# Decoder layer: y's last transposes behind a V sum, query weights split ahead of q's copy, the first half's last additions divided between engines, dt projection of half 1 as one fp32r matmul

## What is computed

```python
# x: (8,128,512), ctx: (8,128,512)
h  = layernorm(x)
xp = h @ xp_w.T                       # 16 columns dt, 16 B, 16 C
dt = softplus(xp[..., :16] @ dt_w.T + dt_b)
# scan over the 128 tokens, 16 states a channel
s_t = exp(dt_t * A) * s_{t-1} + dt_t * B_t * h_t ;  y_t = sum_n s_t * C_t + D * h_t
x  = x + y
z  = layernorm(x); z = z * rsqrt(mean(z*z) + eps) * ln_w
q, k, v = z @ w_q.T, ctx @ w_k.T, ctx @ w_v.T      # 32 heads of 128
x  = x + softmax_masked(q k^T + bias) v @ w_out.T
x  = x + x_ln @ W.T + b + sum_e probs[e] * (x_ln @ A_e^T) @ B_e^T
```

## Time and profile before

| | before |
|---|---|
| median of 3 runs | 916.41 us |
| lowest, highest | 914.9, 916.72 us |
| the profiled execution | 916.63 us |
| its span | 914.8 us |
| PE busy | 904.4 us (99%) |
| DVE, ACT, POOL busy | 697.0, 515.9, 663.8 us |
| mean granted TensorE clock | 0.996 |
| the chain that ended last | PE 87%, DVE 10%, POOL 1% |
| PE's waits that the trace names, the longest three | 2.9 us (line 618, for DVE's y), 1.5 us (line 537, at the start), 1.3 us (line 666, for DVE's `q_sb`) |

### The profile page before, as it was taken

How to read it: one execution, slowest core, us unless ns; L and a number is a source line. 1 busy time by engine, 2 the same in 40 slices (tenths; PEclk the granted TensorE clock), 3 DMA queues, 4 the chain that set the end, 5 groups by cost and what they waited for, 6 DMA issues and landing times.

```text
span 914.8 us, 15425 instructions
## 1 busy us (share of the span) xinstructions
PE 904.4 (99%) x5150; PEld 778.9 (85%) x5150; DVE 697.0 (76%) x763; ACT 515.9 (56%) x1188; POOL 663.8 (73%) x429
## 2 busy tenths in 40 slices
PE   9999999999999998999999999999999999999998
PEld 8687688888888887888899999999899999999876
DVE  5699997999999999456666676676666677767774
ACT  3686868576665675365655555555555555555330
POOL 3247788997678776457698878788878888787522
PEclk9999999999999999999999999999999999999999
DMA  9555476675777753356554444545454545454302
GB/s 310 166 156 166 143 230 184 204 208 183 215 238 229 241 171 126 110 170 226 162 169 157 137 158 135 158 136 158 137 159 135 158 135 160 134 169 136 109 1 93
DMA packets 96849, 150.26 MB, mean 164 GB/s; under 512 B 10576, under 2 KB 35280, under 8 KB 96672
## 3 DMA queue, kind: packets, MB, share of 16 engines
q1 hardware_dynamic: 86432, 131.54, 44.3%
q10 hardware_dynamic: 10368, 18.09, 7.9%
HBM read 113.81 MB, written 35.78 MB: 164 GB/s over the span
## 4 chain that ended last, share of the span: by engine, by line
PE 87%; DVE 10%; POOL 1%; issue 1%; ACT 0%; DVEq 0%; ACTq 0%; POOLq 0%
PE acc L508 11%; PE acc L510 11%; PE acc L509 11%; PE misc L510 6%; PE misc L508 6%; PE misc L509 6%; PE acc L789 6%; PE acc L734 6%; PE acc L666 5%; PE acc L667 5%; PE acc L668 5%; DVE misc L1225 4%; PE acc L758 3%; DVE w L1232 2%; DVE misc L1220 2%
## 5 line engine op out<-in xcount | busy, mean ns | idle before, releaser
L1486 POOL TENSOR_TENSOR y<-y,w 128x2048 f32<-128x2048 f32 x31 | 143.5, 4630 | 58.4 <-DVE w L1232 57.4
L1225 DVE TENSOR_TENSOR_SCAN misc<-dA,misc 128x2048 f32<-128x2048 f32 x32 | 141.7, 4429 | 4.3 <-ACT dA L862 1.1
L1083 ACT ACTIVATE prob<-prob,negm 128x128 f32<-128x128 f32 x256 | 99.9, 391 | 41.6 <-DVE negm L1295 41.6
L1090 ACT ACTIVATE ot_hi<-acc 128x512 fp32r<-128x512 f32 x64 | 38.3, 599 | 143.3 <-PE acc L789 143.3
L1547 POOL TENSOR_TENSOR wt_lo<-ws,wt_hi 128x1024 fp32r<-128x1024 f32 x27 | 65.1, 2410 | 61.7 <-ACT wt_hi L1071 61.7
L508 PE MATMUL misc<-wo_hi,ot_hi 128*128 128x512 f32 x256 | 107.1, 418 | 0.5 <-POOL wo_lo L1564 0.5
L510 PE MATMUL misc<-wo_hi,ot_lo 128*128 128x512 f32 x256 | 101.3, 396 | 0.0
L508 PE MATMUL acc<-wv_hi,ctx_hi 128*128 128x512 f32 x256 | 101.2, 395 | 0.0
L509 PE MATMUL misc<-wo_lo,ot_hi 128*128 128x512 f32 x256 | 100.8, 394 | 0.0
L510 PE MATMUL acc<-wv_hi,ctx_lo 128*128 128x512 f32 x256 | 100.0, 391 | 0.0
L509 PE MATMUL acc<-wv_lo,ctx_hi 128*128 128x512 f32 x256 | 99.9, 390 | 0.0
(11 more groups left out here) (196 smaller groups left out, 2438.6 us busy)
## 6 DMA issues: line engine op xcount, KB each, us to landing
k_scratch<-kst SPq DMA_DIRECT2D x64, 256.0 KB, 3.6
bc<-xp_scratch ACTq DMA_DIRECT2D x32, 512.0 KB, 5.7
v_scratch<-vst SPq DMA_DIRECT2D x32, 512.0 KB, 4.2
k_sb<-k_scratch SPq DMA_DIRECT2D x64, 256.0 KB, 2.9
v_sb<-v_scratch SPq DMA_DIRECT2D x64, 256.0 KB, 2.7
wo_raw<-in_wo SPq DMA_DIRECT2D x64, 256.0 KB, 2.9
wp<-in_wq SPq DMA_DIRECT2D x54, 256.0 KB, 3.8
wraw<-in_wk SPq DMA_DIRECT2D x32, 256.0 KB, 5.0
```

The source lines that it names most:

```text
L1083: last = act.activation(prob[q][:, b], prob[q][:, b], ACT.Exp, bias=negm[q][:, b:b + 1], accum_out=psum[q][:, b:b + 1])
L1225: dve.tensor_tensor_scan(h_ps, flat(dA[k % 2][:, :, :, :]), h_ps, 0.0, ALU.mult, ALU.add).then_inc(da_free, 1)
L1486: pool.tensor_tensor(y_half(half), y_half(half), w[:, k % 2], ALU.add).then_inc(y_ready, 1)
```

## The change

Five parts.

1. **dt projection.** In half 1 it was one fp32 matmul over 16 rows. It becomes one fp32r matmul over 96 rows: three blocks at partitions 0, 32 and 64 hold the low part of xp with the rounded dt weights, then rounded with rounded, then rounded xp with the low part of the weights; the rows between are zero. For that POOL sets `dtw` and `xp3` to zero (`rows_set`), SP loads dt_w three times, ACT's `xp_slot` has one copy of 96x512 and three of 16x512 ahead of its copy of 48x512, and POOL has two subtractions of 16x512 (`low_xp`) behind its addition of step 1. PE's first dt projection waits for the second.
2. **T_DT** goes from 85 to 23, by which `due` moves exponentials on ACT and `low_w` on POOL.
3. **V sum ahead of y's last transposes.** V sum 0 of the last group stands ahead of them; four stand between them and z's transposes as before, and one instead of two in `behind(0)`.
4. **`split_wq(g + 1)`** stands ahead of the copy of q on ACT in the plain steps.
5. **Divided additions.** Of the four of `add_sums(0)`, DVE keeps two. For the other two, ACT copies bank times `anykey` to `o_sum`, and POOL adds it to `base`.

```diff
-KZ = 12
-Y_AT = KP
+Y_AT = KP + 1
+KZ = KP + 5
...
-T_SUM, T_TR, T_XP, T_DT, T_EXP = 273, 45, 340, 85, 234
+T_SUM, T_TR, T_XP, T_DT, T_EXP = 273, 45, 340, 23, 234
...
+            sp.wait_ge(rows_set, 1)
+            for i in range(3):
+                sp.dma_start(dtw[32 * i:32 * i + R], a["dt_w"]).then_inc(dtw_in, 16)
...
             def dt_proj(half, c, out):
 
-                return pe.matmul(out, dtw[:, c * P:(c + 1) * P], xp_sb[0:R, half], start=True, stop=True)
+                cols = slice(c * P, (c + 1) * P)
+                if half:
+                    return pe.matmul(out, dtw3[0:R3, cols], xp3[0:R3], start=True, stop=True)
+                return pe.matmul(out, dtw[0:R, cols], xp_sb[0:R, 0], start=True, stop=True)
...
             pe.wait_ge(w_lo_done, 3)
+            pe.wait_ge(xp_lo_done, 1)
             for c in range(C):
                 pe.wait_ge(sum_evac, max(bank_free(DT[c]), XP + 1))
                 dt_proj(1, c, acc[:, bank_of(DT[c])]).then_inc(sum_done, 1)
...
             k_group(NG - 1)
+            v_group(NG - 1, range(1))
             for b in range(HB):
                 pe.wait_ge(y_ready, NSTEP + b)
                 y_transpose(HB + b, misc[:, b]).then_inc(yt_ps, 1)
-            v_group(NG - 1, range(KZ - KP))
+            v_group(NG - 1, range(1, KZ - KP))
...
                         if known(g) and g - 3 == H:
-                            pe.wait_ge(x2_done, b + 1)
+                            pe.wait_ge(*((o_copied, b + 1) if b < 2 else (x2_done, b - 1)))
...
             def behind(g):
                 if g == 0:
                     v_sum(NG - 1, KZ - KP)
-                    v_sum(NG - 1, KZ - KP + 1)
...
             def xp_slot():
-                act.activation(xp_sb[0:RX, 1], bank(XP)[0:RX], ACT.Copy).then_inc(sum_evac, 1)
+                r = bank(XP)
+                act.wait_ge(rows_set, 2)
+                act.wait_ge(dtw_in, 16 * 3)
+                act.activation(dtw3[0:R3], dtw[0:R3], ACT.Copy)
+                for i in range(3):
+                    act.activation(xp3[32 * i:32 * i + R], r[0:R], ACT.Copy)
+                act.activation(xp_sb[0:RX, 1], r[0:RX], ACT.Copy).then_inc(sum_evac, 1)
...
             def step(g, par, half, i):
                 p, pp = par % 2, par // 2 % 2
+                if plain(g + 1):
+                    split_wq(g + 1, 1 - p)
                 if plain(g):
...
                     act.activation(q_sb[0][:, 0:HALF_T], sumX, ACT.Copy).then_inc(c11_done, 1)
-                if plain(g + 1):
-                    split_wq(g + 1, 1 - p)
...
+                if g == H + 2:
+                    copy_sums()
...
+            def copy_sums():
+                act.wait_ge(o_done, H)
+                for b in range(2):
+                    act.activation(o_sum[:, b], misc[:, b], ACT.Copy, scale=anykey[:, b:b + 1]).then_inc(o_copied, 1)
...
-                for b in range(HB):
+                for b in range(HB) if half else range(2, HB):
                     i = half * HB + b
                     dve.scalar_tensor_tensor(base[:, i], misc[:, b], anykey[:, i:i + 1], base[:, i], ALU.mult,
                                              ALU.add).then_inc(x2_done, 1)
...
+            def low_xp():
+                pool.wait_ge(sum_evac, XP + 1)
+                pool.wait_ge(y_ready, 2)
+                pool.tensor_tensor(dtw3[64:64 + R], dtw[64:64 + R], dtw3[64:64 + R].bitcast(F32), ALU.subtract).then_inc(dtw_hi_done, 1)
+                pool.wait_ge(dtw_hi_done, 1)
+                pool.tensor_tensor(xp3[0:R], xp_sb[0:R, 1], xp3[0:R].bitcast(F32), ALU.subtract).then_inc(xp_lo_done, 1)
+                pool.wait_ge(xp_lo_done, 1)
...
                 pool.tensor_tensor(y_half(half), y_half(half), w[:, k % 2], ALU.add).then_inc(y_ready, 1)
+                if k == 1:
+                    low_xp()
...
+                if g == H + 2:
+                    pool.wait_ge(base_mixed, HB)
+                    for b in range(2):
+                        pool.wait_ge(o_copied, b + 1)
+                        pool.tensor_tensor(base[:, b], base[:, b], o_sum[:, b], ALU.add).then_inc(x2_pool, 1)
```

More of the change, by code:

```diff
@@ L50 @@
 B_AT = 2
+R3 = 96
 ENTRY = 12
@@ L140, in decoder_layer @@
         h_ps = misc[:, :, :].rearrange("p c t -> p (c t)")
+        with ExitStack() as proj:
+            xp_sb = sb(proj, "xp_sb", [P, 2, HT])
+            xp3 = sb(proj, "xp3", [P, HT], F32R)
+            dtw3 = sb(proj, "dtw3", [P, D], F32R)
         base = sb(whole, "base", [P, B, D])
@@ L158, in decoder_layer @@
             xpw = sb(first, "xpw", [P, C, RX])
-            dtw = sb(first, "dtw", [R, D])
+            dtw = sb(first, "dtw", [P, D])
             maskraw = sb(first, "maskraw", [P, B, S], U8)
@@ L208, in decoder_layer @@
         ffn_w = sb(whole, "ffn_w", [P, C, D])
-        sb(whole, "bc_end", [P, 2, HT])
+        o_sum = sb(whole, "o_sum", [P, 2, D])
         with ExitStack() as second_raw:
@@ L276, in decoder_layer @@
         ln1_done = sem("ln1_done")
+        xp_hi_done, xp_lo_done, dtw_in = sem("xp_hi_done"), sem("xp_lo_done"), sem("dtw_in")
+        rows_set, dtw_hi_done = sem("rows_set"), sem("dtw_hi_done")
         xt_ps, xt_evac, xp_ps, xp_evac, dt_ps = sem("xt_ps"), sem("xt_evac"), sem("xp_ps"), sem("xp_evac"), sem("dt_ps")
@@ L374, in _ @@
             sp.dma_start(y_tok[:, 0:HB], a["x"][0:HB].rearrange("b t d -> t b d")).then_inc(x_in[0], 16)
-            for dst, src in ((negA, "A_log"), (dskip, "D"), (dtb, "dt_b"), (xpw, "xp_w"), (dtw, "dt_w"), (lnw, "ln_w")):
+            for dst, src in ((negA, "A_log"), (dskip, "D"), (dtb, "dt_b"), (xpw, "xp_w"), (lnw, "ln_w")):
                 sp.dma_start(dst[:], a[src]).then_inc(params_in, 16)
+            sp.wait_ge(rows_set, 1)
+            for i in range(3):
+                sp.dma_start(dtw[32 * i:32 * i + R], a["dt_w"]).then_inc(dtw_in, 16)
             def k_store(g, j):
@@ L574, in _ @@
             k_sum(0, 5)
-            pe.wait_ge(params_in, 16 * 7)
+            pe.wait_ge(params_in, 16 * 6)
             pe.wait_ge(xt_evac, HB)
@@ L579, in _ @@
             pe.wait_ge(xp_evac, 1)
+            pe.wait_ge(dtw_in, 16 * 3)
             for c in range(C):
@@ L808, in _ @@
                     if b == HB - 1:
-                        f_input(1, *((x2_done, HB + c + 1) for c in range(C)))
+                        f_input(1, *((x2_done, 2 + c + 1) for c in range(C)))
                     tok = slice(b * S, (b + 1) * S)
@@ L924, in _ @@
             split_w(1, wv_hi)
-            act.wait_ge(params_in, 16 * 7)
+            act.wait_ge(params_in, 16 * 6)
             act.activation(negA[:], negA[:], ACT.Exp).then_inc(a_exp, 1)
@@ L1100, in behind @@
                 if g == 0:
-                    for j in range(KZ, KZ + 2):
-                        v_copy(NG - 1, j - KP)
+                    v_copy(NG - 1, KZ - KP)
                     act.wait_ge(z_evac, C)
@@ L1351, in moments_3 @@
             def moments_3(half):
-                dve.wait_ge(x2_done, (half + 1) * HB)
+                dve.wait_ge(x2_done, half * HB + 2)
+                dve.wait_ge(x2_pool, 2)
                 moments(base, half)
@@ L1417, in _ @@
                                pattern=[[-1, P]], channel_multiplier=1).then_inc(ident_done, 1)
+            pool.memset(dtw[0:R3], 0.0).then_inc(rows_set, 1)
             for c in range(C):
@@ L1506, in _ @@
             low_w(2, wk_hi, wk_lo)
+            pool.memset(xp3[0:R3].bitcast(F32), 0.0).then_inc(rows_set, 1)
             added = 0
```

4 lines of the change are left out of this document (2 added, 2 removed).

## The result

| | before | changed |
|---|---|---|
| median of the runs, us (lowest to highest) | 916.65 (914.9 to 920.01), 20 runs | 913.77 (911.61 to 915.81), 20 runs |
| profiled execution, us | 916.63 | 915.79 |
| its span, mean granted clock | 914.8, 0.996 | 914.0, 0.993 |
| busy in it, us: PE, DVE, ACT, POOL | as shown above | 902.8, 699.9, 518.0, 670.7 |

The ratio is 0.9973, with an interval from 0.9964 to 0.9982: about 2.5 to 2.9 us faster, where 5.1 were forecast. 913.77 lies inside the stated range (909.2 to 914.2), near its slow end; the place where the missing part went is not among the rivals.

What follows compares the result with a forecast made beforehand. Up to 364 us DVE's scan sets the end, behind it PE, which is busy 99%. Gains of 0.5 + 2.7 + 0.6 + 1.3 = 5.1 us from 916.6 give 911.5, as median 911.3; range 909.2 to 914.2.

Steps and rivals of the forecast that it cites:

- It is free for PE and worth 0 at the end: dt projections: 3.3 us of PE work saved ahead of the wait for y, bringing nothing at the end.
- it still idles about 3 us: PE ahead of y's transposes: reaches the wait at 360.6, idles about 3 us, which covers PE's earlier losses.
- dt's pitch: dt projections on PE: one fp32r matmul at 0.23 us, saving 0.8 each and 3.3 for four.
- Scan of step 5: DVE's scan in step 5: starts at about 101.7, 0.6 us later than before, released by an exponential.
- The 1.08 wait goes: End of the first half: the scan's 1.08 us wait for an exponential behind a wk split disappears, -1.1.
- DVE's -0.5: DVE up to y: +0.6 at step 5 and -1.1 at the first half's end, so y's transposes start near 363.8.
- V sum, -2.7: Behind y's transposes: one of two V sums leaves behind(0) and fills idle time ahead of y, 2.7 us faster.
- The clock stays up at y: Rival, behind the wait for y: full clock saves 1.5 us on transposes and V sums, giving 909.8; 17%.
- The loop's entry: q of steps 1 and 2: POOL's low parts could come late, 0 to 1.8 us lost; 0 taken.
- Query weights, -0.6: PE's 0.55 us wait for wo_lo at 455.27 goes as wq's split comes earlier; -0.6, bounds 0 and 0.8.
- Divided additions, -1.3: Start of the second half: two fewer DVE additions save 1.36 us, removing PE's 1.28 us wait at 656.19.
- DVE comes to y later than before: Rival, at y: DVE's -0.5 turns to +0.6 or more, giving 912.4 to 914.5; 20%.

Runs made afterwards that it cites:

- e12: The changed kernel run once more, unaltered, for a second profile: 913.57 us, ratio 0.9966 to before.
- e1: The changed kernel with POOL making wv_lo of weight group 3 one addition to y earlier: 910.08 us, ratio 0.9933 to before.
- e9: The kernel before with only wv_lo of weight group 3 put one addition (4.6 us) later on POOL: 918.44 us beside 916.87, ratio 1.0021.
- e4: The changed kernel with the V sum ahead of y's last transposes undone: 916.17 us, ratio 0.9993 to before.
- e6: The kernel before with only the V sum moved ahead of y's last transposes: 914.51 us beside 916.28, ratio 0.9987.
- e10: e1 without the divided additions: 910.82 us, ratio 0.9933 to before.
- e11: e1 with POOL's two divided additions one step later: 910.17 us, ratio 0.9929 to before.

## Why the prediction was right and wrong

**The step that failed** is "It is free for PE and worth 0 at the end, because PE only comes to the wait for y earlier", with "it still idles about 3 us, and this is also the cover of everything that PE might lose ahead of it". I looked for what PE gains up to y and took it to get there. Between 93 and 361 us PE changes weights eleven times (K of group 2 to K of group 7), and at two of these places, V of group 3 and V of group 5, POOL was ready only 0.3 us before PE. No list of waits shows such a margin, because nobody waited. `T_DT` moved the second out of the way, not the first. There PE came 3.2 us early in e12 and POOL 1.2 us late (the scan's delay of step 5); less the margin of 0.3 that is about the stop of 3.85. It spent the cover of 3 us, and 1.7 to 2.4 us of slow clock came on top: PE was forecast at y at 360.6 and came at 366.75, where 3.85 + 1.7 and 0.3 for the later start make 366.5. e1 and e9 show the stop from both sides: taking it away is worth 3.6 to 3.9 us, and putting it into before costs 1.4 to 1.5, since before had 2.9 us of idle time and a slow stretch at y to give for it.

The account of e12 against before, both at 0.996 with one early slow stretch and one of its own, by rows (negative is earlier; 0.3 of the first row is the later start):

| | forecast | measured |
|---|---|---|
| y's transposes on PE: 364.35 to 366.75 | -0.5 | +2.4 |
| V sum | -2.7 | -2.7 |
| clock held behind y | 0 (a rival) | -1.3 |
| query weights | -0.6 | -0.8 |
| divided additions | -1.3 | -0.9 |
| sum | -5.1 | -3.3 |

The last matmul of the kernel moved by 3.2 (911.19 to 907.99).

- **dt's pitch** 0.23: right, but the saving was under-sized. Before, the V sums with a dt slot between them start 4.00 us apart (92.22, 96.22), in e1 2.97 (91.46, 94.43): 1.0 for each slot and 4.1 in all, for 3.3, because the sum behind an fp32 slot also starts slower. Even without the stop the saving does not reach y whole. In e1 PE is ready for y at 362.03, 2.1 us earlier than before's 361.26 with the V sum's 2.73 and e1's later start of 0.13 added; part of the missing 2 us are waits of 0.17, 0.36 and 0.53 us for ACT's copies and a `wk_lo`.
- **POOL's two subtractions**, put at 1.35 each, took 1.30 and 1.29; `wv_lo` of group 1 held by 0.8 us, for 0.9.
- **Scan of step 5**: 103.68, but step 4 already stood 1.79 late in that execution, so 101.89 on before's scale, for 101.7: right; in e12 it is 102.35. **The 1.08 wait goes**: right, but "I add both" fell, as the late copies of B took its place.
- **DVE's -0.5** without the stop: in e1 DVE comes to y 2.0 us earlier on before's scale: +0.8 in step 5, -1.0 in step 24, -1.75 by the normalisation behind step 26, and small ones. The first two terms were right; the third was missing.
- **V sum, -2.7**: right. From transposes to q the changed kernel takes 20.56 us, e4 without the part 23.23: 2.7. The remaining 24.55 - 23.23 = 1.3 is the clock, which did not fall where PE came later and stood 1.5 us or less. The rival *The clock stays up at y* had 1.5 for it; it came true by the road it names, PE later than I thought, but the changed kernel pays for it with the slow stretch behind the stop. e1, where PE waits only 0.49, has it too: 383.01 - 362.52 = 20.49.
- **The loop's entry** at 0 lost: right, and e6 shows the wait of 0.8, and 1.2 us lost in all, that come without part 4.
- **Query weights, -0.6**: 0.79 by the place of the earlier trace rows, the upper bound; the wait there is gone.
- **Divided additions, -1.3**: mechanism right, size off, 0.86. The prediction watched `wt_lo`, which held. What it left out is DVE's product, 1.24 us for 0.77 before: POOL's `bm` now runs under it. The 1.36 us that DVE saves, less these 0.47, make 0.89. The prediction told of contention between DVE and POOL for the additions only; these rows say that it fell on DVE's side: without part 5 the product took 0.78 at this place (e10), and with the additions one step later 1.35 (e11).
- *DVE comes to y later than before* gave the time nearest to the result (912.4 to 914.5), but by other mechanisms (step 5's exponential, another item behind the split) than the one that worked. I count it as a miss.

That the time came inside the range is luck: the terms that were overlooked have both signs, and the largest, the stop, is not among the rivals. With the stop gone, e1 is at 910.08 where before is at 916.85 in the median, 6.8 us faster, and 7.1 in like executions. That is more than the forecast of 5.1, by the clock at y and the normalisation, less what part 5 fell short of.

## What to carry to other kernels

Before calling PE work "free up to the next wait", walk the stretch from the saved work to that wait and write down, at each hand-over, how long the data had been ready: the saving survives only up to the smallest margin, unless the producer moves as well. Here one margin of 0.3 us decided, and moving one POOL instruction ahead of two others brought 3.6 to 3.9 us more, beside the change's 3. A stop of PE was paid twice here: the stop, and the slow clock behind it. It also delayed what was queued on ACT behind copies waiting for PE, and with it DVE; that was not paid, because PE came to y later still.

When executions fall into groups by granted clock, find out first which slow stretches a kernel brings itself. Comparing at equal mean clock takes these out of the difference too: it made the stop look like 2.1 us, and e6's gain like 0.4 instead of 2.0.
